# Straight value latents by transposing the rotated key latents, with another order of the opening

## What is computed

```python
q_lat = x @ w_q_down            # 1024 x 192
kv    = x @ w_kv_down           # 1024 x 64, keys and values of all heads come from it
k_rot = rope(x @ w_k_rope)      # 1024 x 64, shared by the heads
# per head: scores from q_lat, kv and rope parts, softmax, then probs @ kv, then the value and output weights
x = layernorm(x + attention)
```

## Time and profile before

| | |
|---|---|
| median of 3 runs | 2584.31 us (2582.13 to 2592.98) |
| the profiled execution | 2582.9 us |
| its span, first to last instruction | 2580.8 us |
| TensorE busy / weight loads | 2364.9 / 2053.6 us, 14333 instructions each |
| VectorE, ScalarE, GpSimd busy | 1773.9, 1459.6, 1568.7 us |
| mean granted clock of TensorE | 0.951 of full speed |

### The profile page before, as it was taken

One profiled execution on the slowest core, in us unless ns is written; L12 is line 12 of the kernel. 1 busy time (PEld: TensorE's weight loads), 2 busy tenths in 40 slices (PEclk: granted clock), 3 DMA queues, 4 the chain that ended last, 5 costly groups with the idle time before them and its releaser, 6 DMA issues. The chain is left out here.

```text
span 2580.8 us, 44531 instructions
## 1 busy us (share of the span) xinstructions
PE 2364.9 (92%) x14333; PEld 2053.6 (80%) x14333; DVE 1773.9 (69%) x3131; ACT 1459.6 (57%) x3978; POOL 1568.7 (61%) x1320
## 2 busy tenths in 40 slices
PE   8899999993899889999899999998999999987998
PEld 7788888882488778888788888887888888875886
DVE  3566656665923269888788888888888888972232
ACT  1466656661043346667666667666676666664432
POOL 2555555630044277887787878878778878751442
PEclk8899999996599989999999999999999999997999
DMA  2101010101000021110111111101101111003000
GB/s 96 31 23 41 23 41 18 33 1 41 0 1 1 29 64 35 47 55 17 57 45 36 47 42 43 44 29 52 54 24 55 37 42 48 23 5 139 1 17 17
DMA packets 41352, 93.75 MB, mean 36 GB/s; under 512 B 4836, under 2 KB 6760, under 8 KB 39808
## 3 DMA queue, kind: packets, MB, share of 16 engines
q1 hardware_dynamic: 41092, 90.55, 10.9%
HBM read 79.78 MB, written 10.75 MB: 35 GB/s over the span
## 5 line engine op out<-in xcount | busy, mean ns | idle before, releaser
L1095 POOL TENSOR_TENSOR a_nf_acc<-a_nf_acc,a_nf_term 128x512 f32<-128x512 f32 (+1 forms) x416 | 588.6, 1415 | 143.0 <-ACT a_nf_term L1189 72.6
L1575 POOL TENSOR_TENSOR f_w_lo<-WGU,f_w_hi 128x512 fp32r<-128x512 f32 x88 | 114.9, 1307 | 347.8 <-ACT f_w_hi L1591 347.6
L1149 ACT ACTIVATE a_probs<-bank,a_dip 128x128 f32<-128x128 f32 (+1 forms) x512 | 208.3, 419 | 199.5 <-DVE a_dip L1430 199.5
L1158 ACT ACTIVATE a_probs<-a_probs,a_share 128x128 f32<-128x128 f32 (+1 forms) x512 | 192.4, 464 | 61.5 <-DVE a_share L1436 61.5
L1076 POOL TENSOR_TENSOR a_qk_lo<-a_straight,a_qk_hi 128x512 fp32r<-128x512 f32 (+1 forms) x160 | 194.3, 1216 | 47.5 <-ACT a_qk_hi L1135 47.5
L63 PE MATMUL bank<-a_wo_hi,a_ot_hi 128*128 128x512 f32 x512 | 212.3, 415 | 0.0
L365 POOL TENSOR_TENSOR a_straight<-a_straight,a_crossed 128x512 f32<-128x512 f32 x64 | 82.4, 1288 | 212.9 <-DVE a_crossed L718 212.9
L1500 DVE TENSOR_SCALAR a_nf_term<-a_nf_unit 128x512 f32<-128x512 f32 (+1 forms) x288 | 203.6, 751 | 3.4 <-DVE a_nf_unit L1483 0.6
L1441 DVE TENSOR_TENSOR a_pt_lo<-bank,a_pt_hi 128x384 fp32r<-128x384 f32 x256 | 140.9, 550 | 93.8 <-ACT a_pt_hi L1166 93.2
L65 PE MATMUL bank<-a_wo_hi,a_ot_lo 128*128 128x512 f32 x512 | 201.3, 393 | 0.0
L64 PE MATMUL bank<-a_wo_lo,a_ot_hi 128*128 128x512 f32 x512 | 201.0, 392 | 0.0
(11 more groups left out here) (247 smaller groups left out, 8633.0 us busy)
## 6 DMA issues: line engine op xcount, KB each, us to landing
a_raw<-in_l_o SPq DMA_DIRECT2D x64, 256.0 KB, 2.6
a_raw<-in_l_vk SPq DMA_DIRECT2D x32, 384.0 KB, 3.1
a_raw<-in_l_ql SPq DMA_DIRECT2D x32, 320.0 KB, 2.9
a_raw<-in_l_ou SPq DMA_DIRECT2D x32, 288.0 KB, 2.8
n_codes<-coded_w SPq DMA_DIRECT2D x8, 1056.0 KB, 13.1
a_raw<-in_l_nr SPq DMA_DIRECT2D x16, 384.0 KB, 3.0
a_nf_raw<-in_w_nf SPq DMA_DIRECT2D x24, 256.0 KB, 2.6
coded_w<-a_nf_acc SPq DMA_DIRECT2D x24, 256.0 KB, 2.0
```

The costliest lines, as they stand in the source:

```text
L1095: pool.tensor_tensor(acc, left, nf_term[:, i % CODE_RING, 0:w], ALU.add).then_inc(nf_added, 1)
L1149: act.activation(probs[:, n % 2, col:col + keys], bank[:, at:at + keys], ACT.Exp, bias=dip[:, n % 2, i:i + 1], accum_out=total[:, n % 2, i ...
L1158: ins = act.activation(cell, cell, ACT.Copy, scale=share[:, n % 2, i:i + 1])
```

## The change

The straight value latents are no longer computed from the input. Once VectorE has written rows 0 to 63 of the key latents to SBUF (`lat_straight`), eight transposes by TensorE turn them into bank 0. The rotated key latents get buffers of their own (`lat_straight`, `lat_cross`), and a new semaphore `lat_low` tells TensorE that VectorE has finished with banks 0 to 3. The order of the opening on TensorE, ScalarE and VectorE becomes: query latents (u = 0 to 3), W0, W1, key latents (u = 4, 5), W2, W3, value latents, A0, A1. The wait for `lat_ready` stands ahead of the scores instead of ahead of W2. GpSimd's and SP's orders are as before.

```diff
--- before.py
+++ after.py
@@ -231,6 +231,7 @@
         LN = QL + LAT + ROPE
         lat_raw, lat_w = sb("lat_raw", [P, KT, LN], F32), pair("lat_w", [P, KT, LN])
         lat_cos, lat_sin = sb("lat_cos", [P, SEQ], F32), sb("lat_sin", [P, SEQ], F32)
+        lat_straight, lat_cross = sb("lat_straight", [P, 2, HALF], F32), sb("lat_cross", [P, 2, HALF], F32)
         lat_units = [(at, h, rows) for at, rows in ((0, P), (P, QL - P), (QL, P)) for h in range(2)]
         lat_dst = [lambda x, h: x[0][:, 0, h], lambda x, h: x[0][0:QL - P, 1, h], lambda x, h: x[1][:, h]]
         SA, SB_, TURN, AV = banks[0:4]
@@ -242,7 +243,7 @@
         lat_landed, lat_w_hi, lat_w_ready = sem("lat_landed"), sem("lat_w_hi"), sem("lat_w_ready")
         lat_done, lat_hi, lat_crossed, lat_rotated = (sem("lat_done"), sem("lat_hi"), sem("lat_crossed"),
                                                       sem("lat_rotated"))
-        lat_ready = sem("lat_ready")
+        lat_low, lat_ready = sem("lat_low"), sem("lat_ready")
         passed = {"pool": sem("passed_pool")}
         landed = [sem("landed0"), sem("landed1")]
         split_hi, split = sem("split_hi"), sem("split")
@@ -397,18 +398,23 @@
 
         @block.scalar
         def _(act):
-            def latents_high():
-
-                for u, (_, h, rows) in enumerate(lat_units):
-                    hi = lat_dst[u // 2]((CQ.hi, KC.hi), slice(h * HALF, (h + 1) * HALF))
-                    if u < 4:
-                        act.wait_ge(lat_done, u + 1)
-                    else:
-                        act.wait_ge(lat_rotated, h + 1)
-                    act.activation(hi, banks[u][0:rows, :] if u < 4 else straight[:, h, :], ACT.Copy)\
-                       .then_inc(lat_hi, 1)
+            def query_latents_high():
+
+                for u, (_, h, rows) in enumerate(lat_units[0:4]):
+                    act.wait_ge(lat_done, u + 1)
+                    act.activation(lat_dst[u // 2]((CQ.hi, KC.hi), slice(h * HALF, (h + 1) * HALF)), banks[u][0:rows, :],
+                                   ACT.Copy).then_inc(lat_hi, 1)
+
+            def key_latents_high():
+
+                for h in range(2):
+                    act.wait_ge(lat_rotated, h + 1)
+                    act.activation(KC.hi[:, h * HALF:(h + 1) * HALF], lat_straight[:, h, :], ACT.Copy).then_inc(lat_hi, 1)
+
+            def value_latents_high():
+
                 act.wait_ge(lat_done, 7)
-                act.activation(CV.hi[:, :, LAT:2 * LAT], banks[6][:, :].rearrange("p (t r) -> p t r", t=TT), ACT.Copy)\
+                act.activation(CV.hi[:, :, LAT:2 * LAT], banks[0][:, :].rearrange("p (t r) -> p t r", t=TT), ACT.Copy)\
                    .then_inc(lat_hi, 1)
 
             def body(g, first, last):
@@ -463,10 +469,14 @@
                     names = l0_units(True, False)[0:PAIRS + 2]
                     for t in range(TT):
                         high_tile(act, XT, banks[t % 4], signals, 0, t)
+                    query_latents_high()
                     for name in names[0:2]:
                         unit_high(name)
-                    latents_high()
-                    for name in names[2:]:
+                    key_latents_high()
+                    for name in names[2:4]:
+                        unit_high(name)
+                    value_latents_high()
+                    for name in names[4:]:
                         unit_high(name)
                 for n in range(L0_STEPS):
                     exps(n)
@@ -490,20 +500,24 @@
 
         @block.tensor
         def _(pe):
-            def latents():
-
-                pe.wait_ge(signals[2], TT)
-                pe.wait_ge(lat_w_ready, 1)
-                for u, (at, h, rows) in enumerate(lat_units):
+            def latents(units):
+
+                for u in units:
+                    at, h, rows = lat_units[u]
                     for k in range(KT):
                         last = product(pe, banks[u][0:rows, :], lat_w[:, k, at:at + rows],
                                        XT[:, k, h * HALF:(h + 1) * HALF], k == 0, k == KT - 1)
                     last.then_inc(lat_done, 1)
-                pe.wait_ge(ring_free, 1)
+
+            def value_latents():
+
+                pe.wait_ge(lat_low, 1)
                 for t in range(TT):
-                    for k in range(KT):
-                        last = product(pe, banks[6][:, t * LAT:(t + 1) * LAT], XT[:, k, t * P:(t + 1) * P],
-                                       lat_w[:, k, QL:QL + LAT], k == 0, k == KT - 1)
+                    h, col = divmod(t, TT // 2)
+                    if col == 0:
+                        pe.wait_ge(lat_crossed, h + 1)
+                    last = pe.transpose(banks[0][:, t * LAT:(t + 1) * LAT], lat_straight[0:LAT, h, col * P:(col + 1) * P],
+                                        ident[0:LAT, 0:LAT])
                 last.then_inc(lat_done, 1)
 
             pe.wait_ge(ident_landed, 16)
@@ -618,12 +632,19 @@
 
                 if first:
                     names = l0_units(True, False)[0:PAIRS + 2]
+                    pe.wait_ge(signals[2], TT)
+                    pe.wait_ge(lat_w_ready, 1)
+                    latents(range(0, 4))
                     for name in names[0:2]:
                         project(name)
-                    latents()
+                    latents(range(4, 6))
+                    for name in names[2:4]:
+                        project(name)
+                    value_latents()
+                    pe.wait_ge(lat_low, 4)
+                    for name in names[4:]:
+                        project(name)
                     pe.wait_ge(lat_ready, 1)
-                    for name in names[2:]:
-                        project(name)
                     pe.wait_ge(tables_round, 2)
                 for n in range(L0_STEPS):
                     scores(n)
@@ -674,29 +695,38 @@
             dve.tensor_copy(mask_r[:, :], mask[:, :]).then_inc(tables_round, 1)
             dve.tensor_copy(ident_r[:, :], ident[:, :]).then_inc(tables_round, 1)
 
-            def latents_low():
+            def query_latents_low():
+
+                for u, (_, h, rows) in enumerate(lat_units[0:4]):
+                    dve.wait_ge(lat_hi, u + 1)
+                    at = slice(h * HALF, (h + 1) * HALF)
+                    hi, lo = (lat_dst[u // 2]((c,), at) for c in (CQ.hi, CQ.lo))
+                    dve.tensor_tensor(lo, banks[u][0:rows, :], hi.bitcast(F32), ALU.subtract).then_inc(lat_low, 1)
+
+            def key_latents_rotated():
 
                 wide = lambda x: x.unsqueeze(1).to_broadcast([x.shape[0], 2, SEQ])
                 two = lambda x: x.rearrange("p (s t) -> p s t", s=2)
                 for h in range(2):
                     dve.wait_ge(lat_done, 5 + h)
-                    bank = banks[4 + h]
-                    dve.tensor_tensor(two(straight[:, h, :]), two(bank[:, :]), wide(lat_cos[:, :]), ALU.mult)
-                    dve.tensor_tensor(two(crossed[LAT:mid, h, :]), two(bank[mid:P, :]), wide(lat_sin[mid:P, :]),
+                    bank, row = banks[4 + h], lat_straight[:, h, :]
+                    dve.tensor_tensor(two(row), two(bank[:, :]), wide(lat_cos[:, :]), ALU.mult)
+                    dve.tensor_tensor(two(lat_cross[LAT:mid, h, :]), two(bank[mid:P, :]), wide(lat_sin[mid:P, :]),
                                       ALU.mult)
-                    dve.tensor_tensor(two(crossed[mid:P, h, :]), two(bank[LAT:mid, :]), wide(lat_sin[LAT:mid, :]),
+                    dve.tensor_tensor(two(lat_cross[mid:P, h, :]), two(bank[LAT:mid, :]), wide(lat_sin[LAT:mid, :]),
                                       ALU.mult).then_inc(lat_crossed, 1)
                     dve.wait_ge(lat_crossed, h + 1)
-                    dve.tensor_tensor(straight[LAT:P, h, :], straight[LAT:P, h, :], crossed[LAT:P, h, :], ALU.add)\
+                    dve.tensor_tensor(row[LAT:P, :], row[LAT:P, :], lat_cross[LAT:P, h, :], ALU.add)\
                        .then_inc(lat_rotated, 1)
-                for u, (_, h, rows) in enumerate(lat_units):
-                    dve.wait_ge(lat_hi, u + 1)
+
+            def key_value_latents_low():
+
+                for h in range(2):
+                    dve.wait_ge(lat_hi, 5 + h)
                     at = slice(h * HALF, (h + 1) * HALF)
-                    hi, lo = (lat_dst[u // 2]((c, k), at) for c, k in ((CQ.hi, KC.hi), (CQ.lo, KC.lo)))
-                    src = banks[u][0:rows, :] if u < 4 else straight[:, h, :]
-                    dve.tensor_tensor(lo, src, hi.bitcast(F32), ALU.subtract)
+                    dve.tensor_tensor(KC.lo[:, at], lat_straight[:, h, :], KC.hi[:, at].bitcast(F32), ALU.subtract)
                 dve.wait_ge(lat_hi, 7)
-                dve.tensor_tensor(CV.lo[:, :, LAT:2 * LAT], banks[6][:, :].rearrange("p (t r) -> p t r", t=TT),
+                dve.tensor_tensor(CV.lo[:, :, LAT:2 * LAT], banks[0][:, :].rearrange("p (t r) -> p t r", t=TT),
```

(10 more changed lines are left out.)

## The result

The changed kernel takes 2551.68 us (median of 4, 2551.29 to 2555.63), the kernel before 2586.02 us (median of 4): a ratio of 0.9863 with a 95% interval of 0.9845 to 0.9882. The forecast was 2565.9 us with a range from 2556 to 2573.

The account below looks back on a forecast made before the run. TensorE is busy nearly always from the first attention steps, so only the first scores' start counts. Terms (a) to (g) move it from 73.3 to 54.9 us: 2584.3 - 18.4 = 2565.9 us, range 2556 to 2573.

Parts of the forecast that it names:

- (a): Opening: the wide latents no longer stand behind W0 and W1 and start at 17.95 us instead of 21.70.
- (b): Opening: the 48 query-latent products take 12.32 us, six at the low clock, ending at 30.27; upper end 2.5 us more.
- The late clock: Rival, 0.17: clock rises late or breaks in the opening, gain 15.9 to 11.8 us; transposes don't count as clock activity.
- (c): Opening: W0 and W1, now in the middle, take 1.93 us at the high clock, ending at 32.20.
- (d): Opening: 24 key and rotary latent products take 5.60 us, ending at 37.80; the splits for W2 and W3 stay hidden.
- (e): Opening: second half of the keys is rotated, then evicted ahead of W2; A0 may start at 42.5 us.
- (f): Opening: the eight transposes take 1.7 us, ending at 41.8, hidden; at the upper end A0 starts 2.7 us later.
- (g): Opening, A0 to first scores: 12.39 us at the low clock, so scores at 54.9; at the high clock 51.9.
- the first one: Opening claim on the bound: everything behind the first scores (73.30 us) follows in the same order, so only their start counts.
- the rivals: High clock (0.17), late or broken clock (0.17), opening a chain of evictions at low clock (0.08), slower than before (0.03).
- The comparison of the isolated price of a narrow product: Opening: the skill's gap prices the 96 removed products at 2.8 us, the trace at 16.0; the trace was taken.
- The high clock: Rival, 0.17: clock stays high through A0 and A1, scores at 51.9, gain 21.4 us, up to 27.4 through step 1.

Follow-up runs that it names:

- e1: The changed kernel plus 88 small transposes nobody reads, at the head of TensorE's dequantising stage (176 instructions with weight loads); 2562.95 us.
- g2: The changed kernel plus idle 512-column products on TensorE, 6 behind the value latents' transposes and 16 behind A1; 2548.57 us.
- e3: The changed kernel with the 96 narrow value-latent products kept where the transposes stand, so only the order changes from before; 2583.06 us.
- g1: The changed kernel plus seven idle 512-column products in TensorE's two gaps ahead of the query latents; 2549.36 us.
- e2: The kernel before plus 40 small transposes nobody reads in TensorE's dequantising stage (80 instructions); 2569.51 us.
- f1: The kernel before plus 6 small transposes nobody reads in TensorE's dequantising stage (12 instructions); 2574.15 us.
- f2: The changed kernel plus 80 small transposes nobody reads in TensorE's dequantising stage (160 instructions); 2555.90 us.
- e4: The kernel before with eight transposes in place of the 96 narrow value-latent products, every order kept; 2561.36 us.

## Why the prediction missed, step by step

- (a) Start of the wide latents: 18.55, not 17.95. The handoff was as said; the whole opening of this execution ran 0.6 us later, from the input's transposes on.
- (b) The 48 products took 13.78 us, not 12.32. Twelve of them ran at the low pace (18.55 to 23.84). The lower end of the bound had been taken; the upper was 14.8. e1 needed 12.7, g2 12.9, e3 14.0 with the same work ahead, so this varies from one execution to the next, and why isn't shown; g1 shows that wide products ahead of them bring the rise forward (11.3 us). The late clock's sentence on transposes doesn't hold in this case: in e2, with nothing but transposes on TensorE ahead, the last eight of the input took 1.26 us instead of the 1.96 before, and the granted clock reads 1.00 up to 16.1 us and then 0.50 (f1: 1.45 us, f2: 1.55). So the input's transposes did bring the clock up there, and it fell again before the wide products. The row of e2 (before: 14.58 us, 1.96 long):

```profile
15.11 1.26 PE L129 MATMUL bank<-ident,X 128*128 128x128 f32 x8 [2.87 <-DVE XT_lo L145]
```

The Trainium skill (TensorE: Matmul & The Clock Gate, "Part 4: PE-mode transpose") says that the clock's high level doesn't engage for them; these runs differ, and they decide.
- (c), (d) 1.95 and 5.67 us against 1.93 and 5.60. W2 and W3 ran without a wait for a split, as worked out.
- (e) From the last wide product to A0 4.75 us against 4.7. (f) The transposes took 0.88 us for eight, half the price taken, and were hidden. (g) 12.39 us, as forecast, with the low clock in A0 and A1: the window above shows 0.50.
- The sum for the first scores, 54.9 against 57.09, so 16.2 us of gain for 18.4. Step 0 gave back 0.8: the clock came up in it, at about 61.7 us, and not in step 1.
- The step that failed is the first one, "Everything after it hangs on it in the same order as before", and its echo at the sum, that nothing else than the clock's moment differs. It put everything behind the first scores at nothing. The order did stay; but a shorter program puts each later loop elsewhere in TensorE's program, and the five jumps back of the second attention cost 11.2 us less. None of the rivals had that. Without it and the last 2.6 us, which no term had either, the gain is 17.0 us and the time some 2569, within the range. The rows were in the trace of before: two idle stretches of TensorE released by "issue" at each of five jumps. It was not read because it lies outside the edited stage.
- The comparison of the isolated price of a narrow product (2.8 us for 96) with the row (16.0) came out for the row: in e3, the same 96 products took 17.8 us in another place. As a price of the change, though, 16.0 isn't what taking them out is worth: alone, it moved the first scores by 8.2 us (e4).
- The high clock did not come by itself. g2 shows its price up to the scores (3.6 us earlier, against 54.9 - 51.9 = 3.0 in the forecast); for the whole it was too high.

What stays open is how the last 2.6 us come about. Some 1.1 lie around the transfers of the coded weights, and 1.5 at the last stage's head, where 24 products took 7.25 us before and 5.71 after. That is the clock: it reads 0.56 in the first 3.7 us of them before and 1.00 after. It isn't likely to be chance either: these 24 products took 7.25 or 7.26 us in the three kernels with two full stops at each jump (before, e1, e3) and 5.70 or 5.71 in the eight others. So the 1.5 us go with the place in the program too, and what leads from the one to the other isn't shown. Pieces of 1 to 3 us at the first attention's jump came and went between executions.

## What to carry to other kernels

When an edit changes how many instructions stand ahead of a loop, look at the rows behind each jump back, whether the edit touches the loop or not: two stops released by "issue" a few instructions apart were here the sign that the loop's place is a bad one, and a dozen idle instructions in a stage where the engine waits anyway removed the second. Before crediting an edit with a gain, compare the same event in both traces at several places; a constant difference that suddenly steps belongs to something else. And an eviction that only the last consumer needs should not stand ahead of work on the path.

## What the runs showed of the hardware that was not expected

- TensorE stopped for 1.6 to 3.5 us at every jump back of the second attention, and for a further 2.2 to 2.7 us two or three products later in the three kernels with the loop's start within one instruction of the same place. Twelve instructions more ahead (f1) took 11 us off the median, 8.2 of them at the five jumps. Why a first stop takes 1.6 us at one jump and 3.5 at the next isn't shown.
- Idle products in the gaps are worth it in the opening: 29 of them, beside work of other engines, took 5.7 to 7.5 us off.
- The granted clock in the windows reads 1.00 for the first wide products of the changed kernel, though they came 0.427 us apart, the pace of 1.2 GHz; in g2 the same stretch reads 0.50. At the start of an execution the pace of the rows tells the level, the column may not:

```profile
18.50:23.80 5.30, 5.25 (x12) 4.13 (x13) 1.90 (x2) 0.00 (x0) 1.81 (x2) 1.00 0.45 144
```
